# Two-layer graph attention on one Trainium2 core: two quarters of the probabilities turned by DMA, exps in another order, row sums by a column of ones

## What is computed

```python
# layer 0
agg = (mask @ x) / max(deg, 1)
x = layernorm(x + relu(concat(x @ W_self + b_self, agg @ W_nb + b_nb) @ W_comb + b_comb))
# layer 1
value = neigh @ Wv + bv                                  # 4096 x 128
ws = leaky_relu(x_att(x) @ neib_att(neigh).T)            # 4096 x 4096, x_att and neib_att: tanh layers of width 32
ws = softmax(where(adj > 0, ws, NEG_BIG), axis=1)
out = concat(x @ Wfx + bfx, ws @ value)
x = layernorm(x + out)
```

## The kernel before

| slot | TensorE (each also aggregates 8, scores, weighs) | ScalarE (each also leaky, last or nearly) | VectorE (each also masked scores, first or nearly) |
|---|---|---|---|
| 0 | x1 turn | exp 1st; mean | degrees; mask |
| 1 | turn; mean turn | x1 copy; exp 2nd; p_high | row_scale; mask; p_low |
| 2 | turn | mean split; exp 3rd; p_high | layer1; x1_low; p_low |
| 3 | turn; hidden, fx | wide_high; p_high; normalise2 | mean_low; mask; p_low |
| 4 | turn; combine | tanh; exp 4th; p_high | tanh_low; wide_low; p_low |
| 5 | turn; x attention | p_high | layer0; p_low |
| 6 | turn | xatt copy; p_high | stack, fx; p_low |
| 7 | | normalise1 | row_max; mask |

## Time and profile before

### The profile page before, as it was taken

One profiled execution on the slowest core, in us unless ns is written; L12 is line 12 of the kernel. 1 busy time (PEld: TensorE's weight loads), 2 busy tenths in 40 slices (PEclk: granted clock), 3 DMA queues, 4 the chain that ended last, 5 costly groups with the idle time before them and its releaser, 6 DMA issues.

```text
span 730.6 us, 20042 instructions
## 1 busy us (share of the span) xinstructions
PE 690.8 (95%) x7344; PEld 592.1 (81%) x7344; DVE 623.3 (85%) x1567; ACT 584.1 (80%) x1048; POOL 116.1 (16%) x241
## 2 busy tenths in 40 slices
PE   5989998999999999999999999999999999998775
PEld 4646676888888888888888888888888888886554
DVE  4887668999999999999999999999999999987874
ACT  2455248888888888888888988888888888889885
POOL 0010111111111111111111111111111111111201
PEclk9989999999999999999999999999999999999999
DMA  8966999999999999999999999999999999841111
GB/s 269 371 146 162 228 283 220 189 204 234 195 191 211 222 207 208 210 225 210 225 205 209 215 197 218 187 193 234 204 199 218 211 219 224 168 68 35 37 47 44
DMA packets 260147, 141.40 MB, mean 194 GB/s; under 512 B 225361, under 2 KB 243665, under 8 KB 260049
## 3 DMA queue, kind: packets, MB, share of 16 engines
q1 hardware_dynamic: 259604, 140.10, 88.0%
q10 hardware_dynamic: 444, 0.02, 0.0%
HBM read 81.35 MB, written 4.19 MB: 117 GB/s over the span
## 4 chain that ended last, share of the span: by engine, by line
PE 86%; ACT 5%; DVE 4%; issue 3%; POOL 1%; DMA 1%; SPq 0%; ACTq 0%; POOLq 0%; DVEq 0%
PE ps_v L1137 21%; PE ps_agg L1093 15%; PE ps_agg L1096 14%; PE ps_t L1117 11%; PE ps_s L1108 7%; PE ps_agg L1156 3%; PE ps_agg L1159 3%; PE ps_s L1007 2%; PE ps_v L1015 2%; ACT score L915 2%; PE ps_t L998 1%; PE ps_x L1176 1%; PE ps_x L1179 1%; PE ps_x L1024 1%; PE ps_agg L1147 1%
## 5 line engine op out<-in xcount | busy, mean ns | idle before, releaser
L1093 PE MATMUL ps_agg<-x,mask_t 128*128 128x257 f16 x1024 | 243.2, 273 | 0.0
L1096 PE MATMUL ps_agg<-x,mask_t 128*128 128x256 f16 x1024 | 237.3, 273 | 0.3 <-DVE x L527 0.3
L908 ACT ACTIVATE score<-ps_s,sc 128x512 f32<-128x512 f32 x256 | 178.5, 697 | 55.7 <-PE ps_s L1108 51.9
L686 DVE CUSTOM_DVE_ANT_0 score<-score,mask 128x512 f32<-128x512 f32 x256 | 176.0, 687 | 13.3 <-ACT score L908 13.1
L1137 PEld LDWEIGHTS ps_v<-v,late 128*128 128x128 f16 x2304 | 143.3, 97 | 39.0 <-DVE late L750 16.7
L1137 PE MATMUL ps_v<-v,late 128*128 128x128 f16 x2304 | 160.1, 219 | 10.8 <-DVE late L750 5.9
L915 ACT ACTIVATE score<-score,exp_bias,sc 128x1024 f32<-128x1024 f32 x128 | 159.3, 1245 | 3.2 <-DVE exp_bias L695 3.2
L750 DVE TENSOR_TENSOR late<-ps_t,late 128x512 f16<-128x512 f32 x192 | 131.3, 684 | 31.9 <-ACT late L922 30.5
L922 ACT CAST late<-ps_t 128x512 f16<-128x512 f32 x192 | 114.4, 596 | 19.2 <-PE ps_t L1117 19.2
L1117 PE MATMUL ps_t<-ident,score 128*128 128x128 f32 x768 | 118.4, 277 | 7.3 <-ACT score L915 7.3
L1096 PEld LDWEIGHTS ps_agg<-x,mask_t 128*128 128x128 fp8e4 x1024 | 100.2, 98 | 15.6 <-issue 5.2
(11 more groups left out here) (134 smaller groups left out, 822.0 us busy)
## 6 DMA issues: line engine op xcount, KB each, us to landing
adj_sb<-in_adj_dram SPq DMA_DIRECT2D x128, 512.0 KB, 5.4
neigh_sb<-in_L_gnn_neigh_dram SPq DMA_DIRECT2D x8, 512.0 KB, 7.9
score<-in_x_dram SPq DMA_DIRECT2D x8, 512.0 KB, 8.5
x_in<-in_x_dram SPq DMA_DIRECT2D x32, 128.0 KB, 2.6
out_dram<-out_sb SPq DMA_DIRECT2D x32, 128.0 KB, 3.4
mask_t<-mask SPq DMA_TRANSPOSE x128, 4.7
neigh_sb<-neigh_sb SPq DMA_TRANSPOSE x64, 3.7
mask<-in_L_gnn_W_comb_dram SPq DMA_DIRECT2D x1, 512.0 KB, 8.5
```

The source lines that it names most:

```text
L686: dve.tensor_tensor_reduce(score[:, b % 2, part], score[:, b % 2, part], mask[:, b % MASK_BUFS, part], 1.0, -3.0e38, ALU.subtract, ALU.max ...
L908: act.activation(score[:, b % 2, k * GW:(k + 1) * GW], ps_s[k % 2][:, :], ACT.Prelu, alpha=SLOPE, scale=score_scale).then_inc(leaky_made, 1)
L1093: mm = pe.matmul(agg[:, 0:D + 1], mask_t8[:, c, 0, :], x16[:, c, X_HI:X_ONE + 1], start=(c == 0), stop=(c == NC - 1), skip_group_check=True)
L1096: mm = pe.matmul(agg[:, 0:D], mask_t8[:, c, 0, :], x16[:, c, X_LO:X_LO + D], start=False, stop=False, skip_group_check=True)
```

## The change

Two quarters of each block are now split wide and turned by DMA, and four groups by TensorE. Each wide quarter has its own copy, difference, semaphores and buffers (`wide_p[:, w]`, `wide_t[:, w]`, in the memory of `neigh_sb`). The exps run in the order 0, 1, 2, 3 of the quarters and keep no accumulator. The turns start in slot 35 and weighing in slot 36, where it was 33 and 34; the wide quarters are copied in slots 33 and 35, their differences made in 34 and 36, turned in 35 and 37 and weighed in 40, 41 and 42, 43. `v16` gets a column of ones behind its high half, so `ps_v[:, 128]` collects the row sum in 129-column matmuls; `row_scale` is gone and its reciprocal and product stand at the head of `layer1` (slot 44). The statistics of layer 1 and `norm2` move to slot 46, `normalise2` to 47, the store to 48.

```diff
-TURN_AT = 33
-WEIGH_AT = 34
+TURN_AT = 35
+WEIGH_AT = 36
 BY_DMA = 2
-BY_PE = NG - BY_DMA
-EXPS_OF_WIDE = 2
-EXPS = ((0, 1), (1, 0), (2, 2), (4, 3))
-WIDE_HIGH_AT = 35
-WIDE_LOW_AT = 36
-WIDE_TURN_AT = 37
-LAYER1_AT = 42
-SLOTS = NG * (NB - 1) + LAYER1_AT + 1
+BY_PE = NG - 2 * BY_DMA
+EXPS = ((0, 0), (1, 1), (2, 2), (4, 3))
+EXP_PLACE = [[quarter for _, quarter in EXPS].index(k) for k in range(4)]
+WIDE_HIGH_AT = (33, 35)
+WIDE_LOW_AT = (34, 36)
+WIDE_TURN_AT = (35, 37)
+WIDE_WEIGH_AT = (40, 42)
+LAYER1_AT = 44
+NORM2_AT = 46
+SLOTS = NG * (NB - 1) + NORM2_AT + 1
...
-            def turn_wide(b):
-                sp.wait_ge(wide_lo_made, b + 1)
+            def turn_wide(b, w):
+                sp.wait_ge(wide_lo_made[w], b + 1)
                 at_least(sp, pv_done, NG * b)
-                for h in range(BY_DMA):
-                    part = slice(h * CQ, (h + 1) * CQ)
-                    sp.dma_start_transpose(wide_t[:, :, :, :].rearrange("p a c n -> p (a c) n")[:, part, :],
-                                           wide[:, h * QW:(h + 1) * QW]).then_inc(wide_t_in, 16)
+                for half in range(2):
+                    sp.dma_start_transpose(wide_t[:, w, half, :, :], wide_p[:, w, half, :]).then_inc(wide_t_in[w], 16)
...
+            pool.memset(v16[:, :, V_ONE:V_LO], 1.0).then_inc(consts_ready, 1)
...
-                at_least(act, l1_step, 6 * (b - 2) + 1)
                 part = score[:, b % 2, q * QW:(q + 1) * QW]
-                act.activation(part, part, ACT.Exp, bias=exp_bias[:, b % 2:b % 2 + 1], scale=score_unit,
-                               accum_out=sums[:, b % 2, q:q + 1]).then_inc(exp_made, 1)
+                act.activation(part, part, ACT.Exp, bias=exp_bias[:, b % 2:b % 2 + 1],
+                               scale=score_unit).then_inc(exp_made, 1)
...
-                if d := due(s, WIDE_HIGH_AT, 0):
-                    wide_high(d[0])
+                for w, at in enumerate(WIDE_HIGH_AT):
+                    if d := due(s, at, 0):
+                        wide_high(d[0], w)
...
                 if d := due(s, MEAN_AT, 0):
                     mean_of(d[0])
-                if d := due(s, LAYER1_AT + 1, 0):
+                if d := due(s, NORM2_AT + 1, 0):
                     normalise2(d[0])
...
-            def row_scale(b):
-                base = 6 * b
-                dve.wait_ge(exp_made, NQ * (b + 1))
-                dve.tensor_reduce(row2[:, 0:1], sums[:, b % 2, :], AX.X, ALU.add).then_inc(l1_step, 1)
...
             def layer1(b):
...
+                dve.reciprocal(row2[:, 1:2], ps_v[:, V_ONE:V_ONE + 1]).then_inc(l1_step, 1)
+                dve.wait_ge(l1_step, base + 1)
+                dve.tensor_scalar(row2[:, 2:3], row2[:, 1:2], v_inv, None, ALU.mult).then_inc(l1_step, 1)
+                dve.wait_ge(l1_step, base + 2)
...
-                    for part, (p, v) in enumerate(((hi, 0), (hi, DV), (lo, 0))):
-                        mm = pe.matmul(ps_v[:, 0:DV], p, v16[:, c, v:v + DV],
+                    for part, (p, v, n) in enumerate(((hi, 0, DV + 1), (hi, V_LO, DV), (lo, 0, DV + 1))):
+                        mm = pe.matmul(ps_v[:, 0:n], p, v16[:, c, v:v + n],
                                        start=(j == 0 and u == 0 and part == 0),
-                                       stop=(j == NG - 1 and u == CG - 1 and part == 2))
+                                       stop=(j == NG - 1 and u == CG - 1 and part == 2), skip_group_check=True)
...
-                if d := due(s, WEIGH_AT):
-                    weigh_values(*d)
+                if d := turned_by_pe(s, WEIGH_AT):
+                    weigh_values(*d[0:2])
+                for w, at in enumerate(WIDE_WEIGH_AT):
+                    if (d := due(s, at)) and d[1] < 2:
+                        weigh_values(d[0], BY_PE + 2 * w + d[1])
```

More of the change, by code:

```diff
@@ L181, in gnn_kernel @@
         exp_bias = sb("exp_bias", [P, 2], F32)
-        sums = sb("sums", [P, 2, NQ], F32)
         row2 = sb("row2", [P, 4], F32)
@@ L405, in _ @@
             for s in range(0, SLOTS + 3):
+                for w, at in enumerate(WIDE_TURN_AT):
+                    if d := due(s, at, 0):
+                        turn_wide(d[0], w)
                 for q, at in enumerate(MASK_SLOTS):
@@ L518, in v_low @@
                 dve.wait_ge(v_hi_made, turn + 1)
-                dve.scalar_tensor_tensor(out=v16[:, part, DV:2 * DV],
+                dve.scalar_tensor_tensor(out=v16[:, part, V_LO:VW],
                                          in0=ps_s[turn % 2][:, :].rearrange("p (u n) -> p u n", u=TR), scalar=v_scale,
@@ L1111, in turn_p @@
             def turn_p(b, j, n):
[L1112 to L1113 removed]
+                k = 2 * BY_DMA + j
+                pe.wait_ge(exp_made, NQ * b + EXP_PLACE[k // 2] + 1)
                 at_least(pe, p_lo_made, n - 1)
```

89 lines of the change are left out of this document (44 added, 45 removed).

## The result

The change is slower: **757.68 us** (752.67 to 764.48, median of four runs) against 731.57 (731.31 to 731.85), ratio 1.033 (1.031 to 1.0349). The ratio compares means and leaves out the execution of 764.48 as a slow one, whose granted TensorE clock is 0.976 over the run where that of 752.67 has 0.988. The profiled execution took 757.78 us, its span is 756.0, 25.4 more than before. The forecast was 749.8, the range 736 to 758. The median falls 0.3 us inside the range's upper end, and 7.9 above the forecast; one of the four runs lies outside the range, so that the median lies inside it is in part luck.

The account below looks back on a forecast made before the run. The prediction took a 19.54 us loop through ScalarE and TensorE as the bound. +0.60 per period over 27 periods (+16.2) and +1.8 at the ends made +18.0 on 731.82: 749.8 us, range 736 to 758.

Parts of the forecast that it names:

- step (6): DMA and SP queue: two more transposes per block land well before they are weighed; cost 0.
- the loop: First exp to third turn to slot 7's score matmul to next first exp, through ScalarE and TensorE: 19.54 us, forecast 20.14.
- (1): TensorE, slots 1 and 2: two groups of four transposes fewer, 0.88 us per block, worth 0 in the loop.
- (2): ScalarE from first to third exp, then TensorE's third turn: 6.77 us where 6.66 was, loop 0.11 longer.
- the sign of being right: Check on ScalarE's stretch: it is wrong if first exp to third turn is not 6.8 us.
- (4): ScalarE, slot 7: normalise2, moved from slot 3 to between leaky and first exp, adds its whole 0.49 us per period.
- (3): TensorE from third turn to first score matmul: 11.88 us as before; the 129th column taken as nothing, at most 0.04 per block.
- (5): VectorE's loop from slot 2's masked scores to exp_bias: 19.66 to perhaps 19.85 us, under 20.14, so it costs nothing.
- third rival: DMA becomes the bound, 2.7 us on top of every period: up to +73 us, 805; chance 0.04.
- (7): Filling period, three later periods and the end of the run: together +1.8 us.
- first rival: TensorE's own work is the bound, so all 0.88 us per block count: 709.8 us; chance 0.10.

Follow-up runs that it names:

- a_turn_together: The changed kernel with the first pair of DMA turns two slots later, so that both pairs stand in slot 5; 749.98 us, ratio 1.0259.
- b_norm47: The kernel before with normalise2 alone moved from slot 3 to slot 7, and its store four slots later; 738.6 us, ratio 1.0093.
- b_sum_ones: The kernel before with only the row sums changed: a column of ones in the values, no accumulator read behind the exps; 729.97 us, ratio 0.9972.
- a_norm_later: The changed kernel with normalise2 alone six slots later, in slot 4, and its store behind it; 759.31 us, ratio 1.0378.
- b_two_more: The kernel before with two spare DMA transposes per block, issued behind the existing pair in slot 5; 733.89 us, ratio 1.0023.
- a_two_bufs: The changed kernel with a second buffer for the DMA-turned quarters, so SyncE need not wait for the weighing of the block before; 766.24 us, ratio 1.0445.
- a_adj_pool: The changed kernel with the 120 later loads of adj issued from POOL's queue instead of SP's; 895.24 us, ratio 1.2074.
- b_two_early: The kernel before with two spare DMA transposes per block, of the values, issued in slot 3; 759.12 us, ratio 1.0377.

## Why the prediction was right, and where it was not

The direction and the loop held, and the range held by 0.3 us. The forecast was 7.9 us low. The late landings that step (6) put at nothing cost more than that, 10.0 us with the clock; a period forecast 0.08 too long (2.2 us) and the earlier first exp (1.3) hid part of it. By its own sign the forecast fell: it was to fall "if matmuls wait for neigh_sb by DMA", and they waited 26.4 us. The range held because it had been left "a few microseconds of late landings" above a sum that had none.

- **The loop.** The forecast period was 20.14, measured 20.06, over 27 periods 14.0 us where +16.2 stood; it closes at 6.63 + 11.93 + 1.50. TensorE is busy for 18.82 of the 20.06, 94% where 92 to 93 was expected, and VectorE for 17.54, under the 18. With the late landings removed (a_turn_together) the run takes 749.98 us. That this is the forecast to 0.2 us is partly luck: it holds a half-speed stretch in the filling period (1.6) that the forecast did not have, and a period 0.08 shorter.
- **(1), TensorE's 0.88 worth nothing**: right. In a_turn_together TensorE waits 43.2 us, 31 times, for the exp ahead of its third turn, 1.4 each (1.25 in a steady period); about 1.5 was forecast.
- **(2), ScalarE's +0.11**: mis-sized. First exp to third turn was to be 6.77 (the sign of being right said 6.8) and is 6.63, 0.03 less than before and not 0.11 more. 0.04 of the miss is in the rows (5.32 for 5.36); 0.10 is the third exp's accumulator read, which I left in: from the start of that exp to the turn it is 1.41 in before and b_norm47, with the read, and 1.31 in the changed kernel, without it.
- **(2) and (4) as prices, normalise2's +0.49**: right as a row (0.50 for 0.49), wrong as the cost of a step. Step (2) already had the leaky's wait gone, and only normalise2 made it go. By themselves normalise2 costs 0.17 in the changed kernel and 0.29 in the one before, and the rest +0.35.
- **(3), the 129th column**: taken as nothing, bounded at 0.04; it measures about 0.1 a block in b_sum_ones, above my bound. Half of it stands in the loop of the change (11.93 for 11.88), the other half is hidden by the wait ahead of the third turn.
- **(5), VectorE's loop at 19.66 to 19.85**: its mechanism right, its size low: 19.91 in a_norm_later. As forecast it costs nothing while normalise2 stands where it does.
- **(6), "Cost 0"**: the step that failed. I gave both pairs 8 us from issue to use and took the issue to come when the data is ready. The second pair was ready 12 us before its use (448.8 to 460.8) and waited 8.7 of them in the queue. I had counted what the two new transposes hold on the engines and not what stands ahead of them in the one queue, nor that they issue more slowly behind mask turns and loads. Cost in the profiled execution: 8.0 us by nine waits, and 1.6 by the clock behind one of them, a term that the forecast does not have at all. The third rival, DMA as the bound in every period, was wrong in kind: the same bytes cost 0.2% in b_two_more.
- **(7), +1.8 at the ends**: filling -0.46 (forecast -0.4), later periods +0.85 (+0.5), end +2.2 (+1.65), together +2.6; the first exp's earlier start offsets 1.3.
- **The first rival, TensorE's own work**, fell as a forecast of the change, and was nearer than I thought as a description of the kernel before. The rule of the Trainium skill (Perfetto Trace Analysis, Identifying the Most-Contended Engine) named an engine that was busy for all of its period; taking 0.88 us of work off it gained nothing, since a loop 0.11 to 0.16 us longer stood behind it. Both limits were nearly the same, so one had to shorten both.

What stays open: why a transpose issues in 1.23 to 1.31 us at one place of the queue and in up to 3.86 at another; why a_two_bufs waits longer than the change; which part of a_adj_pool costs; and why TensorE's clock falls behind some of its waits and not behind others. That last one may be what moves single executions, since those of the change lie between 752.67 us at a granted clock of 0.988 and 764.48 at 0.976; a difference of a few microseconds between two changed kernels is not to be read from one run of each.

## What to carry to other kernels

Two limits that agree within one or two tenths of a microsecond look like one engine that is 100% busy: look for the small gaps on that engine before taking work off it, and price a step by the wait that it fills as well as by its row. A DMA that compute waits for is dated from when its queue reaches it, not from when its data is ready; put it where few loads and turns stand ahead, even if that is a slot later. And when a step leaves one engine's tight stretch, look whose stretch it enters: the wide copy moved back by one slot put its difference into VectorE's. A wait on TensorE can cost more than itself: read the granted clock behind it before putting all of a long period down to the wait.

## What the runs showed of the hardware

- Durations of the issue of one transpose of 128 by 1024 in f16 by place (tile rows: minimum/median/maximum in ns). The spare pair behind mask turns and adj loads:

```profile
L382 SPq DMA_TRANSPOSE neigh_sb<-v x64: 1231/2248/3857, 119.2 to 736.2; - x64
L374 SPq DMA_TRANSPOSE neigh_sb<-neigh_sb x64: 1231/1310/2588, 127.4 to 746.3; - x64
```

  The first row is b_two_early's pair in slot 3, the second its pair in slot 5.
- A queue share of 98.6% (a_turn_together) to 101.5% (the change) of 16 engines did not tell whether compute waits for a DMA: TensorE waits 1.6 us for turned quarters in the first and 26.4 in the second.
- An accumulator read behind an exp is a row of 0.2 us and costs 0.09; an engine that waits for the exp also starts later by it (TensorE's turn 1.41 after the exp's start with the read in before, 1.31 without it in the change). A 129th column in eight of a group's twelve matmuls costs about 0.01 us a group (0.68 to 0.69 for 0.67).
- TensorE's granted clock fell from 1.00 to 0.50 just behind a wait of 2.02 us in the change and of 2.64 in a_turn_together, and was 1.00 again at 323 and at 124 us, with TensorE at work in between; each fall cost about 1.6 us. Five waits of 2.17 to 3.11 in the change left it at 1.00.
